# Band mask and row sums without their own instructions, three normalisations on GpSimd, a new plan of the orders, loads from two queues

## The reference

```python
# first part, per sequence
scores = einsum(q, k) / 8;  scores = where(causal_mask, -1e6, scores)
z = softmax(scores) @ v;    x = layernorm(resid + z @ W_out + b_out)
# second part, per layer (DEPTH = 2)
def _layer(x, ...):
    q, k, v = split(shift_token(x) @ wqkv)
    q, k = rotary_xpos(l2norm(q) * qs, l2norm(k) * ksc)
    # 64 queries see the 64 keys of their window and the 64 before
    mask = (i < j) | (i > j + WINDOW) | (j == -1)
    sim = where(mask, -finfo.max, einsum(q * 8, k))
    x = x + (softmax(sim) @ v) @ wo
    h = layernorm(shift_token(x)) * lg + lb
    a, g = split(h @ w1 + b1)
    x = x + (a * gelu(g)) @ w2 + b2
# around both: layernorm(x + second part(x))
```

## Time and profile before

| | before |
|---|---|
| time of three runs, us | 1340.97, 1345.1, 1346.7 (median 1345.1) |
| time of the profiled execution, us | 1344.1 |
| its span, us | 1342.0 |
| mean granted clock of TensorE | 0.985 |
| PE busy | 94% |
| VectorE busy | 86% |
| ScalarE busy | 71% |
| GpSimd busy | 67% |
| chain that ended last, by engine | PE 72%, VectorE 18%, ScalarE 4%, issue 4%, GpSimd 2% |

### The profile page before, as it was taken

How to read it: one execution, slowest core, us unless ns; L and a number is a source line. 1 busy time by engine, 2 the same in 40 slices (tenths; PEclk the granted TensorE clock), 3 DMA queues, 4 the chain that set the end, 5 groups by cost and what they waited for, 6 DMA issues and landing times.

```text
span 1342.0 us, 39529 instructions
## 1 busy us (share of the span) xinstructions
PE 1265.5 (94%) x15712; PEld 944.3 (70%) x15712; DVE 1154.8 (86%) x3120; ACT 957.6 (71%) x2596; POOL 903.3 (67%) x765
## 2 busy tenths in 40 slices
PE   6999999999999999999999999999999999999866
PEld 5777767777677776767767776786867777666645
DVE  5799789888999789897899988999899989999764
ACT  5777768787877868678687866877677777866532
POOL 2587588847787487764778675776776847776551
PEclk9999999999999999999999999999999999999978
DMA  5000010000000001000001001000010000000000
GB/s 202 11 17 18 13 25 17 22 6 20 19 22 22 10 17 27 24 14 14 18 17 26 10 17 37 10 21 10 10 29 10 21 10 17 18 17 14 21 13 12
DMA packets 21606, 29.45 MB, mean 22 GB/s; under 512 B 2992, under 2 KB 12080, under 8 KB 21296
## 3 DMA queue, kind: packets, MB, share of 16 engines
q1 hardware_dynamic: 21424, 26.93, 7.8%
HBM read 10.14 MB, written 2.10 MB: 9 GB/s over the span
## 4 chain that ended last, share of the span: by engine, by line
PE 72%; DVE 18%; ACT 4%; issue 4%; POOL 2%; DMA 0%; SPq 0%; POOLq 0%; DVEq 0%; ACTq 0%
PE psum L563 10%; PE psum L590 10%; PE psum L576 5%; PE psum L726 4%; PE psum L599 4%; PE psum L699 4%; PE psum L692 4%; PE psum L664 4%; PE psum L625 3%; PE psum L635 3%; PE psum L538 3%; PE psum L630 3%; PE psum L734 3%; DVE x_hat L1032 3%; DVE prob L904 2%
## 5 line engine op out<-in xcount | busy, mean ns | idle before, releaser
L767 ACT ACTIVATE prob<-prob,negmax 128x512 f32<-128x512 f32 (+3 forms) x512 | 285.0, 559 | 36.7 <-DVE negmax L904 34.5
L904 DVE CUSTOM_DVE_ANT_0 prob<-psum,causal 128x512 f32<-128x512 f32 (+3 forms) x512 | 233.3, 482 | 28.4 <-PE psum L563 26.3
L1101 POOL TENSOR_SCALAR prob<-prob,rowinv 128x384 f32<-128x384 f32 (+1 forms) x256 | 161.8, 647 | 120.7 <-DVE rowinv L910 120.3
L1121 POOL TENSOR_TENSOR rnorm<-ssq,minus_half 128x16 f32<-128x16 f32 x64 | 186.5, 2913 | 57.7 <-DVE ssq L985 56.0
L563 PE MATMUL psum<-k_t,q_t 64*128 64x384 f32 (+3 forms) x1024 | 184.6, 463 | 13.6 <-DVE negmax L904 4.3
L1116 POOL TENSOR_TENSOR r<-r 128x1024 f32<-128x1024 f32 x64 | 151.2, 2363 | 64.0 <-DVE r L949 64.0
L590 PE MATMUL psum<-prob_t,v 128*64 128x128 f32 x2560 | 174.9, 278 | 3.3 <-DVE r L949 1.5
L590 PEld LDWEIGHTS psum<-prob_t,v 128*64 128x64 f32 x2560 | 136.7, 136 | 35.9 <-issue 14.8
L823 ACT ACTIVATE b_prob<-psum,b_negmax 128x128 f32<-128x128 f32 x512 | 145.0, 376 | 22.9 <-DVE b_negmax L977 22.3
L1136 POOL TENSOR_TENSOR b_prob<-b_prob,b_rowinv 128x1024 f32<-128x1024 f32 x64 | 121.6, 1900 | 56.5 <-DVE b_rowinv L995 56.5
L774 ACT COPY prob_t<-psum 128x512 f32<-128x512 f32 (+1 forms) x176 | 96.1, 546 | 77.2 <-PE psum L576 76.0
(11 more groups left out here) (104 smaller groups left out, 2910.7 us busy)
## 6 DMA issues: line engine op xcount, KB each, us to landing
vb_mid<-vb SPq DMA_DIRECT2D x112, 128.0 KB, 2.3
x_t<-in_x_t SPq DMA_DIRECT2D x8, 256.0 KB, 2.9
x_n<-in_x SPq DMA_DIRECT2D x8, 256.0 KB, 2.9
out<-x SPq DMA_DIRECT2D x16, 128.0 KB, 1.8
wqkv<-in_wqkv SPq DMA_DIRECT2D x1, 1536.0 KB, 9.4
w<-in_w SPq DMA_DIRECT2D x1, 682.0 KB, 11.3
wq<-in_wq SPq DMA_DIRECT2D x1, 512.0 KB, 3.7
wout<-in_wout SPq DMA_DIRECT2D x1, 512.0 KB, 5.5
```

The source lines that it names most:

```text
L767: last = af(pr, pr, ACT.Exp, bias=negmax[:, k % 4, o:o + 1], scale=-1.0, accum_out=rowsum[:, k % 4, o:o + 1])
L904: vec.tensor_tensor_reduce(prob[:, k % PROBS, h, p * K:(p + 1) * K], bank[:, p * K:(p + 1) * K], causal[:, S - K:S], -E ** -0.5, 3.0e38, A ...
L1101: last = gp.tensor_scalar(pr, pr, rowinv[:, k % 4, h:h + 1], 1.0, ALU.mult, ALU.mult)
L1121: gp.tensor_tensor(rnorm[:, a, :], ssq[:, a, :], minus_half[:], ALU.pow).then_inc(rnorm_ready, 1)
```

## The change

- The two mask matmuls and the bf16 identity leave `scores_b`. `maxima_b` does for each head what `maxima` does in the first part: one custom operation adds the mask to the 128x128 scores, writes them negated to `b_prob` in SBUF and takes the maximum. It now holds the waits for `p_turned` and for the tables, which the exponentials held.
- The exponentials read `b_prob` in SBUF, and an accumulator gives the row sums; `sums` is gone.
- The normalisations `norm_a` and `end` go from VectorE to GpSimd, and of `norm` the two pieces that come from SBUF; the two from PSUM stay on VectorE.
- Steps that reuse what GpSimd now reads later get waits for it (`residual_a`, `stats`, `end_stats`, `w2_add`).
- The plan gets new prices, signal delays, a pull of 0.00871, a bonus or malus in ns per kind of step (`HURRY`), a shape change at 97 ns, and a sequence in which layer 1 lags by two groups from group 14 on. With it all orders and banks are made anew.
- `x_t` of the first sequence is first on SP's queue, then `wk`, `causal`, `ident`; `wq` in two halves and `wv` are issued by ScalarE. Each has its own semaphore. The tables of the rotation come after the first maxima.

```diff
-BANKS = 8
+BANKS, LATE = 8, 14
...
     groups = TILES // GROUP
-    tiles = []
-    for m in range(groups + 1):
-        for layer, g in ((0, m), (1, m - 1)):
-            if 0 <= g < groups:
-                tiles += [(layer, GROUP * g + k) for k in range(GROUP)]
+    tiles, behind = [], 0
+    for g in range(groups):
+        tiles += [(0, GROUP * g + k) for k in range(GROUP)]
+        last = groups - 1 if g == groups - 1 else g - (2 if g >= LATE else 1)
+        while behind <= last:
+            tiles += [(1, GROUP * behind + k) for k in range(GROUP)]
+            behind += 1
     return tiles
...
-LAG = {"pe": 230, "act": 120, "dve": 100, "pool": 130, "sp": 2300}
-SWITCH, TABLES = 190, 1283
+LAG = {"pe": 230, "act": 230, "dve": 180, "pool": 130, "sp": 2300}
+SWITCH, TABLES, SHY, PULL = 97, 1283, 0, 0.00871
+HURRY = {("act", "a_k"): -100, ("act", "a_q"): 100, ("act", "b_exp"): -400, ("act", "b_gelu"): 1500, ("act", "b_h"): 400,
+         ("act", "b_turn_p"): 400, ("act", "b_turn_qk"): 100, ("dve", "a_y"): 700, ("dve", "b_h"): 100,
+         ("dve", "b_lengths"): -200, ("dve", "b_norm"): 200, ("dve", "b_turn_qk"): 200, ("dve", "b_w2"): 100,
+         ("dve", "end_stats"): -300, ("dve", "tables"): 2900, ("pe", "b_ffn"): 100, ("pe", "b_scores"): 100,
+         ("pool", "a_deviation"): -100, ("pool", "a_norm"): 100, ("pool", "a_scale"): 200, ("pool", "b_deviation"): -100,
+         ("pool", "b_inverse"): -800, ("pool", "b_rotated"): -200, ("pool", "end"): 1700, ("pool", "end_deviation"): -1000,
+         ("pool", "x_res"): 900}
...
-                start = max(free[e], can[k])
+                start, shy = max(free[e], can[k]), 0
                 if e == "pe":
                     if s.frees:
                         start = max(start, by_time[len(s.frees) - 1])
                     if s.mode.split()[0] != mode:
                         start += SWITCH
+                        shy = SHY
                 elif e == "act" and s.mode and s.mode != function:
                     start += TABLES
-                if start < 1e17 and (best is None or start - pull * way[k] < best[0]):
-                    best = (start - pull * way[k], k, start)
+                key = start + shy - pull * way[k] - HURRY.get((e, s.name), 0)
+                if start < 1e17 and (best is None or key < best[0]):
+                    best = (key, k, start)
...
-            for dst, src, signal in ((wq, "wq", proj_in), (wk, "wk", proj_in), (wv, "wv", proj_in), (causal, "causal", causal_in)):
-                sync.dma_start(dst[:], t_in[src]).then_inc(signal, 16)
...
                 sync.dma_start(x_t[:, k, :], t_in["x_t"][b]).then_inc(x_t_in[k], 16)
+                if b == 0:
+                    for dst, src, signal in ((wk, "wk", wk_in), (causal, "causal", causal_in), (ident, "ident", turn_in)):
+                        sync.dma_start(dst[:], t_in[src]).then_inc(signal, 16)
...
-                for s in range(2):
-                    mm(banks[s], ident_b[:], band[:, min(n % NT, 2 - n % 2), :].unsqueeze(1).broadcast_to([P, CB, P]), start=True, stop=True)
...
-                                      seen, start=False, stop=True, skip_group_check=True)
+                                      seen, start=True, stop=True)
...
+            for h in range(2):
+                scalar.dma_start(wq[:, 4 * h:4 * h + 4, :], t_in["wq"][:, 4 * h:4 * h + 4, :]).then_inc(wq_in[h], 16)
+            scalar.dma_start(wv[:], t_in["wv"]).then_inc(wv_in, 16)
...
-                act.wait_ge(tables_ready, LAYERS)
-                act.wait_ge(b_max_ready, nth("dve", "b_max", (l, n, s)))
-                act.wait_ge(p_turned, nth("pe", "b_turn_p", before(l, n, 2)))
-                bank = banks_of("b_scores", l, n)[s]
                 for c in range(CB):
-                    last = af(b_prob[:, a, s, c, :], bank[:, c * P:(c + 1) * P], ACT.Exp, bias=b_negmax[:, a, s * CB + c:s * CB + c + 1])
+                    act.wait_ge(b_max_ready, CB * (nth("dve", "b_max", (l, n, s)) - 1) + c + 1)
+                    pr = b_prob[:, a, s, c, :]
+                    o = s * CB + c
+                    last = af(pr, pr, ACT.Exp, bias=b_negmax[:, a, o:o + 1], scale=-1.0, accum_out=b_rowsum[:, a, o:o + 1])
...
+                dve.wait_ge(x1_ready, nth("pool", "a_norm", tile(NT * b + i - 2)))
...
-            def norm_a(b, i):
-                a = (NT * b + i) % 2
-                dve.wait_ge(rs_a_ready, nth("pool", "a_deviation", (b, i)))
-                g = (NT * (b - 2) + i) // GROUP
-                dve.wait_ge(stored[g % 2], 16 * (g // 2 + 1))
-                vec.tensor_scalar(x1[:, b % 2, i, :], y[:, a, :], mv_a[:, a, 0:1], rs_a[:, a:a + 1], ALU.subtract, ALU.mult).then_inc(x1_ready, 1)
...
+                dve.wait_ge(late_in, 16 * 9)
+                dve.wait_ge(tables_ready, LAYERS)
                 dve.wait_ge(b_scored, nth("pe", "b_scores", (l, n)))
+                dve.wait_ge(p_turned, nth("pe", "b_turn_p", before(l, n, 2)))
                 bank = banks_of("b_scores", l, n)[s]
-                vec.tensor_reduce(b_negmax[:, a, s * CB:(s + 1) * CB], bank.rearrange("p (c n) -> p c n", c=CB),
-                                  AX.X, ALU.max, negate=True).then_inc(b_max_ready, 1)
+                for c in range(CB):
+                    o = s * CB + c
+                    vec.tensor_tensor_reduce(b_prob[:, a, s, c, :], bank[:, c * P:(c + 1) * P], band[:, min(n % NT, 2 - n % 2), :],
+                                             -1.0, 3.0e38, ALU.add, ALU.min, b_negmax[:, a, o:o + 1]).then_inc(b_max_ready, 1)
...
-            def sums(l, n):
+            def inverse_b(l, n):
                 a = PLACE[l, n] % 2
                 dve.wait_ge(b_exp_done, nth("act", "b_exp", (l, n, 1)))
-                vec.tensor_reduce(b_rowsum[:, a, :], b_prob[:, a, :, :, :].rearrange("p s c n -> p (s c) n"), AX.X, ALU.add).then_inc(b_sum_ready, 1)
-
-            def inverse_b(l, n):
-                a = PLACE[l, n] % 2
-                dve.wait_ge(b_sum_ready, nth("dve", "b_sums", (l, n)))
...
+                dve.wait_ge(f_turned, nth("pe", "b_turn_f", group_before(l, g, 2)))
...
-                    for src, e in ((x2[:, l, o + k, 0:E], 0), (bank[:, k * E:(k + 1) * E], E)):
-                        last = vec.tensor_scalar(x_hat[:, k, e:e + E], src, mv_b[:, a + k, 0:1], rs_b[:, a + k:a + k + 1], ALU.subtract, ALU.mult)
-                last.then_inc(x_hat_ready, 1)
+                    last = vec.tensor_scalar(x_hat[:, k, E:P], bank[:, k * E:(k + 1) * E], mv_b[:, a + k, 0:1], rs_b[:, a + k:a + k + 1],
+                                             ALU.subtract, ALU.mult)
+                last.then_inc(x_hat_dve, 1)
...
+                dve.wait_ge(y_out_ready, nth("pool", "end", (g - 2,)))
...
+            def norm_a(b, i):
+                a = (NT * b + i) % 2
+                g = (NT * (b - 2) + i) // GROUP
+                pool.wait_ge(rs_a_ready, nth("pool", "a_deviation", (b, i)))
+                pool.wait_ge(stored[g % 2], 16 * (g // 2 + 1))
+                gp.tensor_scalar(x1[:, b % 2, i, :], y[:, a, :], mv_a[:, a, 0:1], rs_a[:, a:a + 1], ALU.subtract, ALU.mult).then_inc(x1_ready, 1)
...
+            def norm_b(l, g):
+                o, a = GROUP * g % 4, PLACE[l, GROUP * g] % 4
+                pool.wait_ge(rs_b_ready, nth("pool", "b_deviation", (l, g)))
+                pool.wait_ge(f_turned, nth("pe", "b_turn_f", group_before(l, g, 1)))
+                for k in range(GROUP):
+                    last = gp.tensor_scalar(x_hat[:, k, 0:E], x2[:, l, o + k, 0:E], mv_b[:, a + k, 0:1], rs_b[:, a + k:a + k + 1],
+                                            ALU.subtract, ALU.mult)
+                last.then_inc(x_hat_pool, 1)
...
+            def end(g):
+                a = g % 2 * GROUP
+                b, t = tile(GROUP * g)
+                pool.wait_ge(rs_e_ready, nth("pool", "end_deviation", (g,)))
+                for k in range(GROUP):
+                    last = gp.tensor_scalar(x1[:, b % 2, t + k, :], x1[:, b % 2, t + k, :], mv_e[:, a + k, 0:1], rs_e[:, a + k:a + k + 1],
+                                            ALU.subtract, ALU.mult)
+                last.then_inc(y_out_ready, 1)
```

More of the change, by code:

```diff
@@ L324, in sem @@
             return ctx.enter_context(nc.semaphore(name))
-        ident, ident_b = sb("ident", [P, P]), sb("ident_b", [P, P], BF16)
+        ident = sb("ident", [P, P])
         causal = sb("causal", [P, S], BF16)
@@ L438, in load @@
                 if b == 0:
-                    for dst, src, signal in ((ident, "ident", turn_in), (wout, "wout", wout_in)):
-                        sync.dma_start(dst[:], t_in[src]).then_inc(signal, 16)
+                    sync.dma_start(wout[:], t_in["wout"]).then_inc(wout_in, 16)
                     sync.dma_start(bout[:], t_in["bout"].partition_broadcast(P)).then_inc(bout_in, 16)
@@ L505, in emptied @@
                 elif name == "b_scores":
[L506 removed]
+                    pe.wait_ge(b_max_ready, CB * nth("dve", "b_max", (*args, part)))
```

(16 more changed lines are left out.)

141 lines of the change are left out of this document (72 added, 69 removed).

## The result

| | before | after |
|---|---|---|
| median of four runs each, us | 1343.2 | 1265.4 (1263.8 to 1265.7) |
| ratio, 95% interval | | 0.941 (0.939 to 0.944) |
| span of the profiled execution, us | 1342.0 | 1263.6 |

The account below looks back on a forecast made before the run. The prediction took PE, busy 94%, as the bound, with VectorE second. Its terms, 30 + 5 + 22 + 0 + 10 = 67 us, took 1344.1 to 1277 us; range 1250 to 1313.

Parts of the forecast that it names:

- 1, the masks: Second part, 64 tiles: PE loses two mask matmuls each, 30 us of its own work, hidden by nothing (bounds 27 and 34).
- 2, the start: First loads and rotation tables: earlier first matmul and no wait ahead of the first scores, 5 us (bounds 2 and 6).
- 3, VectorE: VectorE loses row sums and normalisations, its maxima cost 21 us more; busy time from 1154.8 to about 1008 us.
- 4, ScalarE: The second part's 512 exponentials get an accumulator read, 55 us more, 1012 us in all, beside a busier PE.
- 5, GpSimd: The moved normalisations cost GpSimd 44 us by the line through its scalings; busy time from 903 to 947 us.
- Rival D: GpSimd's new instructions wait for VectorE at the shared port: 44 us on GpSimd, half on PE's path, 1299 us; chance 0.05.
- Rival B: Moved normalisations in GpSimd's in-order queue delay what PE needs; slower, 1356 or 1403 us by the delay; chance 0.05.
- 6, the orders: New orders and VectorE's relief cut PE's idle time in the body by 22 us, possible 0 to 35.
- the tail: Last 92 us: the new sequence takes back 10 of PE's 28.1 us idle (bounds 25 won, 10 lost).
- the changes of shape: PE's shape changes, 690 counted at 0.1 us: 100 either way are 10 us, taken as 0 (bounds -10 and +25).
- Rival A: The orders give nothing; only masks and start count: 1309 us, up to 1319 with more shape changes; chance 0.17.
- Rival C: More than forecast: body idle nearly vanishes, tail gives 20 us, 100 fewer shape changes; 1244 us, or 1260; chance 0.17.

Follow-up runs that it names:

- e1: The changed kernel in the same orders and banks, with the two mask matmuls of each tile put back on PE; 1290.7 us, ratio 0.960.
- e2: The kernel before in its own orders, with the mask matmuls of the second part left out and nothing in their place; 1325.9 us, ratio 0.988.
- e11: The changed kernel in the same orders, with its loads issued as before, all by SP and the weights first; 1266.0 us, ratio 0.941.
- e5: The changed kernel planned anew with one more dependence, GpSimd's three normalisations back on VectorE; 1301.0 us, ratio 0.967.
- e12: The changed kernel planned anew with one more dependence (1262.9 us), then in those orders VectorE's clip of the sums of squares given to GpSimd; 1248.7 us, ratio 0.928.
- e8: The changed kernel with GpSimd's x_hat multiplying by one pointer and an immediate 1.0, the mean not subtracted; 1263.9 us, ratio 0.939.
- e4: The changed kernel in all its instructions, ordered by the old plan (old prices, delays, pull and sequence, no bonuses); 1309.4 us, ratio 0.974.

## Why the prediction was right, point by point

**1, the masks: right, a little high.** 30 us forecast, 25 measured in the changed kernel (e1), 18 in the old one (e2). The prediction said that no other work hides them; 6 of 31 us are hidden.

**2, the start: right.** 5 us were forecast. PE's idle time in the first 20 us falls from 7.4 + 2.9 to 4.8 us, by 5.4: 2.6 of it ahead of the first matmul (forecast at 5.5 us, seen at 4.82) and 2.9 by the wait ahead of the first scores, which is gone. e11 takes back the loads alone, and 2.5 us of their 3.3 are still there at the end of its profiled execution. No run takes back the place of the tables.

**3, VectorE: right in kind, 47 us off in size.** Forecast 1008 us busy, measured 1054.6. The stalls didn't leave with the normalisations: the clip went from 31.3 to 45.8 us, the other short instructions with operands in SBUF (`ve_b` 12.8 to 17.6, the last residual 9.3 to 11.6) grew too, together 22 us. The maxima follow each other at the forecast 0.21 us. The sum also took out 254.5 us by the groups' own busy times, and those overlap what stands before them on VectorE: counted without that overlap, in the trace of before, the removed groups are 235 us. That explains 20 more. Even so the move of the normalisations is worth 38 us (e5), more than all that the sum had for the body. The page "Perfetto Trace Analysis" of the Trainium skill (Optimizing Scalar/DVE Operations) warned that such a move might not help; here it helped by 38 us, and with e12 by 13 more. The stall itself agrees with the skill's page "SBUF — State Buffer" (SBUF: two separate sides), that the one which starts second waits for the whole instruction of the other: 605.62 beside 605.59 above, with GpSimd first. The other direction, GpSimd waiting for VectorE, shows in none of GpSimd's 64 `x_hat`.

**4, ScalarE: right.** Forecast 1012 us, measured 995.8. The new plan loads tables 58 times and not 68, which saves 10 x 1.28 = 13 us of it. ScalarE is in no large wait of PE but one, 4.5 us for `f_t`.

**5, GpSimd: half.** The line through the scalings gave 44 us, the trace has 87.4. The mis-sized term is the price of the form: scalings with one pointer and an immediate say nothing of a subtraction and a multiplication by two pointers, 582 ns for 317 (e8). It cost no time: e8 takes 19 us off GpSimd and the time stays. Rival D's mechanism, GpSimd waiting for VectorE, is refuted for `x_hat` by its durations, 575 to 594 ns over 64. Rival B didn't come either: PE waits 4.8 us in all for GpSimd in the changed kernel, and 7.2 before.

**6, the orders: the sign right, the place wrong.** 22 us were forecast for the body's idle time. 15.7 came there, 2.9 of which belong to the start, so 12.8. 10 were forecast for the tail, and its idle time fell by 1.3; but the last 92 us now hold 765 matmuls in place of 609, so the window's idle time doesn't measure what the sequence is worth. 0 was forecast for the changes of shape: there are 99 fewer. Each is 0.15 to 0.22 us, twice the prediction's 0.1, since that price looked only at the group behind a change. About 50 of the 99 go with the masks and are in their 31 us (e1); the other 49 make 7 to 11 us. With the masks and up to 6 us for the clock this explains 38 to 48 of the 58.9 us that PE's busy time fell. The remaining 11 to 21 us stay open; stalls shorter than the modelled end of a matmul would count as busy, but no run shows that.

**The sum** came out 11 us short, with misses of both signs, and that it came so near is in part luck. The prediction itself named a fall of PE's busy time far from 30 us as a sign of being wrong, and it was 58.9; the idle time gave 19.5 us where 37 were forecast. By the two traces the 78.4 us are 31 for the masks, 5.4 for the start, 12.8 for the body's idle time, 1.3 for the tail's, 7 to 11 for the other changes of shape, up to 6 for the clock, and 11 to 21 that stay open; forecast were 30, 5, 22, 10, 0 and none for the last two. Rival A's number, 1309, is what e4 measured, but not by its terms: of the 34 us of e4, the masks (18 to 25) and the start (5) leave 4 to 11 for the relief of VectorE, which A put at nothing. Rival C had the number of changes right, 100 fewer, at half their price. What no rival foresaw is that the parts need each other: 9 + 34 isn't 78.

## What to carry to other kernels

When one engine is full and another stands close behind, relief of the second shows in two places, as shorter waits of the first and as less busy time of it, here about half each (e5): count what an order costs (changes of shape, table loads) before and after, and price a change on both of its sides. Remove the short instructions of VectorE that wait for a long GpSimd one, even where GpSimd does them more slowly; look for a mean far above the least duration, and see whether the first engine then waits for GpSimd instead (e12). Compare the granted clock before busy times. And plan anew after each change of content, then try each part alone: here content gave 34 us, the plan 9, both 78.

## What the runs showed of the hardware

- GpSimd's `tensor_scalar` on 128x64 takes 582 ns with a subtraction and a multiplication by two pointers, and 317 ns with one pointer and an immediate; on 128x128 the first form takes 796 ns, so 3.3 ns a column against 0.86.
- A VectorE `tensor_scalar` of 16 columns in SBUF takes 174 ns at best and up to 2065 ns (the changed kernel); one that was looked at ends with the GpSimd instruction beside it. VectorE's custom operation on 128x128 with an operand in PSUM keeps its duration, 230 to 293 ns over 512.
- GpSimd's `x_hat` of the same run doesn't stretch: 575 to 594 ns over 64. Its scalings (L1101) reach 925 ns, against means of 589 and 701; the cause was not looked for.
- A change of shape on PE costs the group ahead of it and the one behind: together 0.15 to 0.22 us.
- At a granted clock of 0.50, two matmuls of 512 bf16 columns take 0.94 us from start to start of the next group, and 0.53 at 1.00. One kernel, e2, ran 1325.0 us at a mean clock of 0.989 and 1335.3 at 0.980.
- An exponential of 128 columns with accumulator keeps ScalarE busy 0.39 us (199.1 us over 512), against 0.28 without; the first reads SBUF and the second PSUM, so the accumulator isn't the only difference.
